# Scales of a batch of groups in four VectorE operations, and the exchange of peaks at another place of the tick

## What is computed

```python
def step(prev_h, xw):                       # layer 0, a plain RNN
    next_h = jnp.tanh(prev_h @ Wh + xw)     # xw = x_t @ Wx + b, 512 wide
    return (next_h, next_h)
...
def step(carry, xw_t):                      # layer 1, an LSTM
    prev_h, prev_c = carry
    a = xw_t + prev_h @ Wh                  # 2048 wide: i, f, o, g
    next_c = f * prev_c + i * g             # i, f, o sigmoids, g tanh of a
    next_h = o * jnp.tanh(next_c)
    return ((next_h, next_c), next_h)
...
x = x + rnn(x, cond_1024)
x = x + lstm(x, cond_1024)
```

## Time and profile before

| what | value |
|---|---|
| median of three runs | 924.98 us |
| the three runs | 925.75, 923.38, 924.98 us |
| the profiled execution's own time | 926.62 us |
| its span, first to last instruction | 924.8 us |
| mean granted clock of TensorE | 0.988 of full speed |
| TensorE, matmuls: busy, instructions | 872.1 us (94%), 17908 |
| VectorE: busy, instructions | 768.0 us (83%), 1992 |
| ScalarE: busy | 404.6 us (44%) |
| GpSimd: busy | 224.6 us (24%) |

### The profile page before, as it was taken

How to read it: one execution, slowest core, us unless ns; L and a number is a source line. 1 busy time by engine, 2 the same in 40 slices (tenths; PEclk the granted TensorE clock), 3 DMA queues, 4 the chain that set the end, 5 groups by cost and what they waited for, 6 DMA issues and landing times.

```text
span 924.8 us, 40894 instructions
## 1 busy us (share of the span) xinstructions
PE 872.1 (94%) x17908; PEld 501.3 (54%) x17908; DVE 768.0 (83%) x1992; ACT 404.6 (44%) x1126; POOL 224.6 (24%) x495
## 2 busy tenths in 40 slices
PE   3799998999999999999899999999899998999996
PEld 2435454455556555556556555656556555656542
DVE  4797795898888888888888888888888888888875
ACT  4454432534444434444444444444444443444431
POOL 1113111112222222222222222222222222222210
PEclk8899998999999999999999999999999999999999
DMA  8900020000101000011011000111000000000000
GB/s 270 293 2 24 2 71 24 25 14 15 26 26 26 26 26 12 17 26 26 26 26 26 15 17 22 26 26 26 25 15 22 19 15 14 15 14 15 15 14 13
DMA packets 40331, 31.34 MB, mean 34 GB/s; under 512 B 4440, under 2 KB 37976, under 8 KB 39000
## 3 DMA queue, kind: packets, MB, share of 16 engines
q1 hardware_dynamic: 40152, 28.72, 11.2%
HBM read 20.32 MB, written 8.39 MB: 31 GB/s over the span
## 4 chain that ended last, share of the span: by engine, by line
PE 69%; DVE 8%; issue 3%; ACT 2%; POOL 1%; POOLq 0%; DVEq 0%; ACTq 0%
PE ps_l L850 28%; PE ps_l L813 27%; PE ps_r L881 7%; PE ps_r L898 6%; DVE xT L512 1%; DVE pre_l L654 1%; ACT gates L446 1%; DVE pre_r L704 1%; POOL xr L353 1%; ACT xr L432 1%; DVE hT_r L721 1%; DVE yT_lo L542 0%; DVE ig L663 0%; DVE fc L661 0%; DVE h_hi L677 0%
## 5 line engine op out<-in xcount | busy, mean ns | idle before, releaser
L333 POOL TENSOR_TENSOR xb<-xb,h_l 128x128 f32<-128x128 f32 x128 | 58.7, 459 | 409.8 <-DVE h_l L682 409.8
L813 PE MATMUL ps_l<-whl_hi,hT_hi 128*32 128x512 f16 x1920 | 126.5, 380 | 6.7 <-DVE hT_hi L680 6.7
L654 DVE SCALAR_TENSOR_TENSOR pre_l<-ps_l,unscale,bias_l 128x256 f32<-128x256 f32 x240 | 104.6, 477 | 30.6 <-PE ps_l L813 25.2
L850 PE MATMUL ps_l<-wxl_hi,yT_hi 128*32 128x512 f16 x1920 | 127.1, 381 | 0.0
L850 PE MATMUL ps_l<-wxl_hi,yT_lo 128*32 128x512 f16 x1920 | 127.1, 381 | 0.0
L850 PE MATMUL ps_l<-wxl_lo,yT_hi 128*32 128x512 f16 x1920 | 127.1, 381 | 0.0
L813 PE MATMUL ps_l<-whl_hi,hT_lo 128*32 128x512 f16 x1920 | 126.0, 379 | 0.0
L813 PE MATMUL ps_l<-whl_lo,hT_hi 128*32 128x512 f16 x1920 | 126.0, 379 | 0.0
L446 ACT ACTIVATE gates<-pre_l 128x256 f32<-128x256 f32 x128 | 53.4, 418 | 127.7 <-DVE pre_l L654 124.7
L704 DVE SCALAR_TENSOR_TENSOR pre_r<-ps_r,unscale_r,xr 64x128 f32<-64x128 f32 x208 | 72.8, 350 | 40.2 <-POOL xr L353 36.3
L881 PE MATMUL ps_r<-whl_raw,wxl_raw 128*32 128x256 f16 x2496 | 88.5, 273 | 10.1 <-DVE wxl_raw L712 10.1
(11 more groups left out here) (103 smaller groups left out, 1282.5 us busy)
## 6 DMA issues: line engine op xcount, KB each, us to landing
xb<-in_x SPq DMA_DIRECT2D x128, 64.0 KB, 2.0
out<-xb SPq DMA_DIRECT2D x128, 64.0 KB, 1.8
wxl_raw<-in_L_cond_Wx SPq DMA_DIRECT2D x5, 1024.0 KB, 18.0
whl_raw<-in_L_cond_Wh SPq DMA_DIRECT2D x4, 1024.0 KB, 10.2
wxl_raw<-in_L_cond_Wx SPq DMA_DIRECT2D x4, 256.0 KB, 4.0
whr<-in_L_cond_Wh SPq DMA_DIRECT2D x4, 256.0 KB, 4.3
bias_l<-in_L_cond_b SPq DMA_DIRECT2D x4, 64.0 KB, 13.7
h0n<-in_cond SPq DMA_DIRECT2D x1, 64.0 KB
```

The source lines that it names most:

```text
L333: nc.gpsimd.tensor_tensor(xb[g % NX][:, t, :], xb[g % NX][:, t, :], h_l[s % 2][:, :], ALU.add).then_inc(out_done, 1)
L654: nc.vector.scalar_tensor_tensor(out=pre_l[:, cols], in0=ps_l[s % 2][:, cols], scalar=1.0 if s < S0 else unscale[:, g:g + 1], in1=bias_l[: ...
L813: last = nc.tensor.matmul(ps_l[s % 2][quarter(j), :], (hT_hi, hT_lo)[h_part][:, k, :], gate_slice(whl[w_part][k], j), start=False, stop=(h ...
L850: last = nc.tensor.matmul(ps_l[s % 2][quarter(j), :], (yT_hi, yT_lo)[y_part][g % 2][:, k, t, :], gate_slice(wxl[w_part][k], j), start=(y_p ...
```

## The change

For a batch, x_power now makes the power of two (two operations) and x_scale makes everything else in two: one product of the power with six factors, each broadcast over the groups, and one reciprocal of all the products. The factors (the unit and the two weight scales, for the LSTM in columns 0 to 2 and for the RNN in 3 to 5) are made once, which adds one operation to weight_scale of the last weights and one to rnn_weight_scale; one that made the unit stays. The products 0 and 3 are unscale and unscale_r, the reciprocals 1, 2, 4 and 5 the scales. Batches from 2 on make all six rows at once; batches 0 and 1 make three, and batch 1's other three follow in x_scale_r.

On VectorE, spread of a batch of tick k moves from the end of the tick to just behind hidden, x_power is at the end of tick k, and x_scale stands behind hidden of tick k + 1. On TensorE, spread_peaks of a batch moves from tick k + 1, behind recurrent_l, to the end of tick k. The exchange of the RNN weights keeps its places. turn_peaks waits for x_power of the batch before, in place of that batch's whole x_scale.

```diff
-        X_STEPS = 6
-        R_STEPS = 5
-        RX_STEPS = 4
+        X_STEPS = 4
+        R_STEPS = 6
+        RX_STEPS = 2
...
+        def rnn_scales(eng, g):
+
+            if batch_of(g) == 1:
+                eng.wait_ge(r_scale_step, RX_STEPS)
+            else:
+                eng.wait_ge(scale_step, X_STEPS * (batch_of(g) + 1))
...
-                act.wait_ge(r_scale_step, RX_STEPS * batch_of(g))
+                rnn_scales(act, g)
...
+            def unit_and_products(first, inverse, scale, done, steps):
+                unit = factors[:, first:first + 1]
+                nc.vector.tensor_scalar(unit, inverse[:, 0:1], inverse[:, 1:2], 2.0 ** -14, ALU.max, ALU.mult).then_inc(done, 1)
+                dve.wait_ge(done, steps + 1)
+                nc.vector.tensor_scalar(factors[:, first + 1:first + 3], scale[:, :], unit, None, ALU.mult).then_inc(done, 1)
...
-                dve.wait_ge(done, X_STEPS * i + 2)
-                nc.vector.tensor_scalar(unscale[:, cols], g_power[:, cols], w_unit[:, :], None, ALU.mult).then_inc(done, 1)
-                dve.wait_ge(done, X_STEPS * i + 3)
-                nc.vector.tensor_scalar(g_inverse[:, 0, cols], unscale[:, cols], w_scale[:, 0:1], None, ALU.mult).then_inc(done, 1)
-                nc.vector.tensor_scalar(g_inverse[:, 1, cols], unscale[:, cols], w_scale[:, 1:2], None, ALU.mult).then_inc(done, 1)
-                dve.wait_ge(done, X_STEPS * i + 5)
-                nc.vector.reciprocal(g_scale[:, :, cols], g_inverse[:, :, cols]).then_inc(done, 1)
...
+            def scales(i, kinds, done, step):
+                first, count = BATCHES[i]
+                cols, shape = slice(first, first + count), [P, kinds.stop - kinds.start, count]
+                nc.vector.tensor_tensor(g_products[:, kinds, cols], g_power[:, cols].unsqueeze(1).broadcast_to(shape),
+                                        factors[:, kinds].unsqueeze(2).broadcast_to(shape), ALU.mult).then_inc(done, 1)
+                dve.wait_ge(done, step + 1)
+                nc.vector.reciprocal(g_inverses[:, kinds, cols], g_products[:, kinds, cols]).then_inc(done, 1)
+
+            def x_scale(i):
+                dve.wait_ge(w_step[OF_X], W_STEPS + 2)
+                dve.wait_ge(scale_step, X_STEPS * i + 2)
+                scales(i, slice(0, 3) if i < 2 else slice(0, 6), scale_step, X_STEPS * i + 2)
+
+            def x_scale_r():
                 dve.wait_ge(r_step, R_STEPS)
...
+                scales(1, slice(3, 6), r_scale_step, 0)
...
                 if 0 <= k - LAG < T:
                     hidden(k - LAG)
+                if k in BATCH_AT:
+                    spread(exchange_x(BATCH_AT.index(k)), BATCHES[BATCH_AT.index(k)][1])
+                if k - 1 in BATCH_AT:
+                    x_scale(BATCH_AT.index(k - 1))
...
-                if k - 1 in BATCH_AT:
-                    x_scale(BATCH_AT.index(k - 1))
+                if k in BATCH_AT:
+                    x_power(BATCH_AT.index(k))
                 if k - 1 == R_SCALE_AT:
                     rnn_weight_scale()
-                    x_scale_r(1)
-                if k - 1 in BATCH_AT[2:]:
-                    x_scale_r(BATCH_AT.index(k - 1))
-                if k in BATCH_AT:
-                    spread(exchange_x(BATCH_AT.index(k)), BATCHES[BATCH_AT.index(k)][1])
+                    x_scale_r()
...
-                if k - 1 in BATCH_AT:
-                    i = BATCH_AT.index(k - 1)
-                    spread_peaks(exchange_x(i), BATCHES[i][1])
...
-                    wait(pe, scale_step, X_STEPS * i)
+                    wait(pe, scale_step, X_STEPS * (i - 1) + 2)
...
-                    pe.wait_ge(scale_step, X_STEPS + 1)
+                    pe.wait_ge(scale_step, X_STEPS + 2)
...
                 if R0 <= k + 1 < T:
                     product_r16(k + 1)
+                if k in BATCH_AT:
+                    i = BATCH_AT.index(k)
+                    spread_peaks(exchange_x(i), BATCHES[i][1])
```

More of the change, by code:

```diff
@@ L98, in rnn_lstm_kernel @@
         w_scale = sb("w_scale", [P, 2])
-        w_unit = sb("w_unit", [P, 1])
         g_bound = sb("g_bound", [P, NG])
         g_power = sb("g_power", [P, NG])
-        unscale = sb("unscale", [P, NG])
-        g_inverse = sb("g_inverse", [P, 2, NG])
-        g_scale = sb("g_scale", [P, 2, NG])
+        factors = sb("factors", [P, 6])
+        g_products = sb("g_products", [P, 6, NG])
+        g_inverses = sb("g_inverses", [P, 6, NG])
         r_peak = sb("r_peak", [P, 2])
@@ L108, in rnn_lstm_kernel @@
         r_scale = sb("r_scale", [P, 2])
[L109 to L112, removed]
+        unscale, unscale_r = g_products[:, 0, :], g_products[:, 3, :]
+        g_scale, g_scale_r = g_inverses[:, 1:3, :], g_inverses[:, 4:6, :]
         OF_H, OF_X = 0, 1
@@ L573, in weight_scale @@
                     dve.wait_ge(w_step[OF_H], W_STEPS)
-                    nc.vector.tensor_scalar(w_unit[:, :], w_inverse[:, 0:1], w_inverse[:, 1:2], 2.0 ** -14, ALU.max,
-                                            ALU.mult).then_inc(done, 1)
-                    dve.wait_ge(done, W_STEPS + 1)
+                    unit_and_products(0, w_inverse, w_scale, done, W_STEPS)
             def rnn_weight_scale():
@@ L587, in rnn_weight_scale, with x_power @@
                 nc.vector.reciprocal(r_scale[:, :], r_inverse[:, :]).then_inc(r_step, 1)
[L588 to L592, removed]
+                unit_and_products(3, r_inverse, r_scale, r_step, 4)
+            def x_power(i):
                 (first, count), done = BATCHES[i], scale_step
@@ L607, in x_scale @@
-                dve.wait_ge(done, X_STEPS * i + 5)
-                nc.vector.reciprocal(g_scale[:, :, cols], g_inverse[:, :, cols]).then_inc(done, 1)
-            def x_scale_r(i):
-                (first, count), done = BATCHES[i], r_scale_step
-                cols, before = slice(first, first + count), RX_STEPS * (i - 1)
-                dve.wait_ge(r_step, R_STEPS)
[L615 to L621, removed]
+            def scales(i, kinds, done, step):
[5 more added lines that the diff above has]
+                nc.vector.reciprocal(g_inverses[:, kinds, cols], g_products[:, kinds, cols]).then_inc(done, 1)
```

## The result

The changed kernel takes 909.28 us, the median of four runs (907.76 to 909.61), against 925.37 us of the kernel before in the same comparison: a ratio of 0.9826, 95% interval 0.9806 to 0.9846. The forecast was 907.4, the range 903.5 to 912.0. The two profiled executions took 926.62 and 909.14 us, 17.5 us apart where the sum said 17.6; the medians are 16.1 apart. Lines behind L98 have other numbers than before: L818 is L813, L855 is L850, L886 is L881, L903 is L898, L912 is L907, L919 is L914, L659 is the cell's L654, L685 is L680, L717 is L712, L709 is L704, L726 is L721, L556 is L551, L560 is L555, L605 and L607 (x_power) are L598 and L600, L358 and L347 are GpSimd's L353 and L342; L613 and L616 are the two new operations of x_scale.

A forecast was written before the change was run, and what follows sets the result against it. TensorE was taken as the bound, with only its pauses to win back. Gains of 10.6 (six later batches), 6.3 (ticks 17 to 20) and 0.7 us (batch 0) sum to 17.6, from 924.98 to 907.4 us; range 903.5 to 912.0.

The forecast's parts named there:

- six later batches: From tick 21 on, TensorE's waits fall from 3.20 to 1.44 us a batch, 10.6 us gained for six.
- ticks 17 to 20: Batch 1 and the exchange of the recurrent weights: L907's wait for L598 goes, 6.3 us gained.
- batch 0: L914 of the first batch no longer waits behind two long weight operations: 0.7 us gained, between 0 and 1.1.
- The first stall stays: TensorE's wait at L914 for VectorE's diagonal moves to the end of tick k: 1.44 us a batch, not 1.34.
- the first stall goes too: Rival, chance 0.04: L914 at the end of tick k never waits, six times 1.44 us less, 898.8 us.
- The second stall goes: In tick k+2, the 1.86 us pause of L881's last eight matmuls, from ten small VectorE operations before the cell, disappears.
- GpSimd holding x_scale: Rival, chance 0.17: behind hidden of tick k+1, x_scale waits for GpSimd's add, 0.1 to 0.2 us beyond margin; 908.1 us.
- a fall at each new stall: Rival, chance 0.03: the clock falls after L914 at the end of tick k, seven times 2.96 us; 928.1 us.

The follow-up runs named there:

- the two halves: Against the kernel before: four operations all at the end of tick k+1, spread and L914 unmoved, 918.10 us; ten old operations at the new places, 914.85 us.

## Why the prediction was right

*The sum.* Its terms, from the two profiled executions:

| term | predicted, us | measured, us | from |
|---|---|---|---|
| six later batches | 10.6 | 10.6 | L813 of tick 21 to the end of the span: 924.8 - 171.56 = 753.24, now 907.4 - 164.80 = 742.60 |
| ticks 17 to 20 | 6.3 | 6.3 | 33.60, now 27.30 |
| batch 0 | 0.7 | 0.9 | turn_peaks of tick 10 to tick 13: 84.51 to 108.02, now 84.96 to 107.57 |
| before tick 10 | 0 | -0.45 | 84.51, now 84.96 |

The last line is the loading of the weights: after, TensorE waits 0.72 us for whr at 13.27. That is no part of the change: in the profiles of the experiments this wait lies anywhere between nothing and 1.3 us.

The four ticks came about as the working said: tick 17 takes 7.80 us (predicted 7.93), tick 18 6.07 (6.06), ticks 19 and 20 13.43 (13.29). But how close the total came is in part luck. The profiled execution of the kernel before is 1.25 us over its median, and its clock fell to 0.53; with a fall as in the kernel with batch 1 undone, 1.3 us less, the 6.3 would be some 5.0 (an estimate from 3.0 and 1.7). The medians' 16.1 us are 1.5 less than the sum.

*The first stall stays.* Predicted 1.44 us, measured 1.45. The reason, that TensorE is early in both orders, is shown by the two kernels that let it come later or the diagonal earlier; both lose the wait and nothing else. What L914 costs without a wait was wrong: the sum counts the 0.31 us behind it, and it is 0.62 in all. That didn't show in the 1.44, since the 0.31 us ahead of L914 pass while TensorE waits. The rival "the first stall goes too" takes off the whole 1.44 and so has L914 at nothing. With 0.62 left its time is 907.4 - 6 x 0.82 = 902.5, not 898.8, and the kernels that do it take 902 and 904. The sign that the prediction gave for this step, L914 waiting 1.1 to 1.5 us at 7 places, holds by the starts (1.14 us at the six later ones) and not by the rows (0.75).

*The second stall goes.* x_scale was put at 0.5 us and took 0.50, and the margin behind it at 0.31 (0.39 less a delay of 0.08), measured 0.30 and 0.29. The delay itself is smaller: L709 follows L886 by 2.21 us (645.80 to 648.01), and by 2.18 in the kernel without x_scale there. The step that carried the forecast, that neither fewer operations nor better places alone would do, was only implicit in the arithmetic; the two halves show it with 3.6 and 4.3 of 10.1 us left by the waits.

*GpSimd holding x_scale.* The rival didn't come about in the changed kernel; the rows of two others show something like it. In the changed kernel product and add start within 0.02 us of each other, the product takes 0.14 us in all six batches, and the add takes 0.48 us instead of 0.46:

```profile
647.49 0.48 POOL L358 TENSOR_TENSOR xr<-xr,bias_r 128x128 f32<-128x128 f32 x1 [0.40 <-ACT xr L437]
```

In the kernel with the four operations at the end of the tick the add was there first, and the product lasts until it has ended:

```profile
658.99 0.45 POOL L347 TENSOR_TENSOR xb<-xb,h_r 128x128 f32<-128x128 f32 x1
659.15 0.32 DVE L613 TENSOR_TENSOR g_products<-g_power,factors 128x24 f32<-128x24 f32 x1
```

In the sixth batch with three reciprocals the add is 0.20 us ahead, and the product again lasts until it has ended (752.87 against 752.84). So where the rows put the add 0.16 and 0.20 us ahead, the product takes 0.32 and 0.29 us, 0.15 to 0.18 us more than 0.14 and not the add's whole 0.46. The changed kernel's rows put the add ahead too, by 0.02 us, and the product takes 0.14; start times on GpSimd are rough in these profiles, so they don't tell which of the two came first there, and no run shows what decides whether the product waits.

*The clock.* It stayed at 1.00 behind the pause of 1.05 us in tick 17, and the six later ones of 0.75 are followed by ticks of 6.50 us. So the rival with a fall at each new stall was wrong. That the clock falls behind L907's pause was right (a mean of 0.53, 0.57 and 0.73 in three profiled executions); that this costs 3.0 us, 6.3 x (1 - 0.53), holds for the profile read the earlier trace rows, not for every execution.

## What to carry to other kernels

When two engines work through fixed lists, moving the exchange on both can leave the wait as long as it was (1.34 us became 1.45). Find which engine is early, move the later one's part up or the earlier one's back, and check the margin of whatever it is moved past; what the exchange itself costs, 0.62 us here, stays. A chain of small operations is worth cutting until it fits the idle time and the margin at its place, and no further: here four operations at the new places lost nothing, four at the old ones or ten at the new ones lost 0.8 to 0.9 us a batch. A description of a change may name a part that costs time; undoing one part at a time finds it.

## What the runs showed of the hardware

A product of 24 elements with both operands broadcast takes 0.14 us, less than the one-tensor product of four elements by a pointer scalar (0.23 us for L609 and 0.22 for L610 in the kernel with the places alone); with 24, 12 and 6 elements it takes 0.14, 0.15 and 0.18 us in the changed kernel, so its time doesn't grow with them there, while the reciprocal's does: 0.19 us with 6, 0.23 with 12, 0.30 with 24. A tensor_scalar on 4 x 4 elements takes 0.22 us alone and 0.41 beside a GpSimd add (L560 ahead of hidden, at 632.32, and in the changed kernel behind it, at 639.83). The small fp32 matmul of four rows by 128 columns costs the stream of tiled matmuls 0.62 us even when its operands have long been there, while turn_peaks (L907 before, L912 after), with 128 rows by four columns, costs about 0.01: tick k of the kernel before takes 6.50 us with it (646.57 to 653.07), where others take 6.49.
